# Row of digits and zero of the scan read from PSUM in a radix ranking, with 20 more indirect DMAs beside it

## The reference, cut to what matters

```
gathered = edge_weight[:, None] * h[src]            # 50000 rows
support  = segment_sum(gathered, dst, num_segments=3125)
```

## Time and profile before

| | before |
|---|---|
| median of 3 runs | 6582.15 us (6579.54 to 6584.24) |
| profiled execution, its time | 6588.37 us |
| its span, first to last instruction | 6586.3 us |
| mean granted TensorE clock | 0.885 |
| busy: TensorE, VectorE, GpSimd, ScalarE | 75%, 43%, 35%, 17% |

### The profile page before, as it was taken

One profiled execution on the slowest core, in us unless ns is written; L12 is line 12 of the kernel. 1 busy time (PEld: TensorE's weight loads), 2 busy tenths in 40 slices (PEclk: granted clock), 3 DMA queues, 4 the chain that ended last, 5 costly groups with the idle time before them and its releaser, 6 DMA issues. The chain is left out here.

```text
span 6586.3 us, 86958 instructions
## 1 busy us (share of the span) xinstructions
PE 4944.6 (75%) x21628; PEld 3310.2 (50%) x21677; DVE 2845.9 (43%) x6136; ACT 1150.8 (17%) x2799; POOL 2318.4 (35%) x2417
## 2 busy tenths in 40 slices
PE   4647498979769795776587767496978797979845
PEld 3424376458624684443265434275877443434433
DVE  5575596032330424566696566695242202020142
ACT  2412252012200121111011111012222101010021
POOL 2787302714345042477531577441024000000015
PEclk9999999978879797889898888698979898989957
DMA  0000133435634164699773699673046342414234
GB/s 15 2 1 13 55 140 147 157 111 177 188 128 134 49 200 129 207 305 306 214 241 108 227 306 306 186 268 100 21 132 196 138 138 84 152 60 163 71 80 130
DMA packets 484461, 952.74 MB, mean 145 GB/s; under 512 B 112783, under 2 KB 292602, under 8 KB 481852
## 3 DMA queue, kind: packets, MB, share of 16 engines
q1 hardware_dynamic: 332508, 642.20, 28.8%
q0 software_dynamic: 114208, 281.05, 14.2%
q10 hardware_dynamic: 37568, 27.34, 1.4%
HBM read 733.91 MB, written 216.46 MB: 144 GB/s over the span
## 5 line engine op out<-in xcount | busy, mean ns | idle before, releaser
L1148 PE MATMUL banks<-ring,xn 128*128 128x512 f32 (+1 forms) x3500 | 1355.8, 550 | 143.7 <-DMA ring<-adjacency 143.7
L1148 PEld LDWEIGHTS banks<-ring,xn 128*128 128x128 f32 x3500 | 630.5, 192 | 870.0 <-issue 724.3
L991 POOL DMA_INDIRECT rows<-pairs,idxr x832 | 811.5, 975 | 239.3 <-issue 216.1
L1881 PE MATMUL banks<-agg,hotT 128*128 x1664 | 639.2, 490 | 229.8 <-issue 219.0
L381 POOL DMA_INDIRECT dst_table<-nodes_pay,nodes_row x392 | 379.6, 968 | 643.8 <-DVEq L1116 476.3
L1881 PEld LDWEIGHTS banks<-agg,hotT 128*128 128x128 f32 x1664 | 305.8, 224 | 514.0 <-issue 505.4
L381 POOL DMA_INDIRECT bin_table<-bins_pay,bins_row x392 | 458.7, 1170 | 269.7 <-DVE bins_row L767 119.1
L1854 DVE TENSOR_TENSOR prod<-banks,rows 128x512 f32<-128x512 f32 x416 | 268.0, 686 | 422.7 <-DMA rows<-pairs,idxr 157.4
L1519 POOL MEMSET second<- 64x8192 f32 x1 | 6.9, 6919 | 1204.2 <-POOLq L130 1204.2
L1056 PE MATMUL banks<-spans,lanes 128*128 128x256 f32 x1440 | 332.9, 388 | 119.3 <-DVE spans L1037 107.2
L2346 DVE TENSOR_SCALAR yT<-banks,bs 128x512 f32<-128x512 f32 (+1 forms) x42 | 27.2, 688 | 879.0 <-PE banks L2327 879.0
(11 more groups left out here) (352 smaller groups left out, 6825.2 us busy)
## 6 DMA issues: line engine op xcount, KB each, us to landing
ring<-adjacency SPq DMA_DIRECT2D x150, 1280.0 KB, 5.8
spill<-rows SPq DMA_DIRECT2D x208, 512.0 KB, 5.5
rows<-spill SPq DMA_DIRECT2D x208, 512.0 KB
w1r<-in_L_ffn_W SPq DMA_DIRECT2D x114, 512.0 KB, 3.7
adjacency<-strips SPq DMA_DIRECT2D x13, 3200.0 KB
w1r<-in_L_ffn_w SPq DMA_DIRECT2D x65, 512.0 KB, 3.8
rows<-home_rows SPq DMA_DIRECT2D x35, 640.0 KB
ring<-adjacency SPq DMA_DIRECT2D x25, 640.0 KB, 3.8
```

The source lines that it names most:

```text
L991: nc.gpsimd.indirect_dma_start(rows[:, row, :], None, table, bass.IndirectOffsetOnAxis(ap=idxr[:, at + g:at + g + 1], axis=0))\
L1148: last = nc.tensor.matmul(K.ps[2 * (g % 2) + o][:, 0:wd], x[:, t * D + o * P:t * D + (o + 1) * P], ring[:, n % R, 0:wd // cols, q * SPAN_S ...
L1881: last = nc.tensor.matmul(K.ps[2 + 2 * (jj % 2) + g // 2][:, g % 2 * D:(g % 2 + 1) * D], hotT[:, jj % 2, g * P:(g + 1) * P], tile_of(q, t) ...
```

## The change

The row of digits is copied from SBUF to PSUM bank 7 at the start of each ranking, with a memset of one column there to zero. All comparisons of L564 read the row from PSUM. The scan reads this zero, repeated, as the operand of its maximum, in place of reading `counts` twice; the running sums are never below zero, so the result is the same. VectorE waits for its own copy (`numbered`) ahead of the first comparison. Two of the shares rise: 38 columns instead of 24 beside stage 0 of the nodes' ranking, and 36 instead of 30 beside stage 1. So 29 are left for the layer norm.

```diff
--- before.py
+++ after.py
@@ -541,6 +541,8 @@
     PARTS = 7
     PER_PART = COLS // PARTS
     BF5 = 5
+    WIDEST = max(L, N)
+    digit_iota, nought = K.ps[7][:, 0:WIDEST], K.ps[7][:, WIDEST:WIDEST + 1]
     fills = -(-NB // BF5)
     with stage(nc) as st:
         lo = st.sb("lo", [P, COLS, L], BF)
@@ -549,7 +551,7 @@
         counts = places[:, :, :, :].rearrange("p b d n -> p (b d n)")[:, 0:N * NB]
         counts3 = counts.rearrange("p (n b) -> p n b", b=NB)
         with stage(nc) as st1:
-            made, counted, kept = (st1.sem(x) for x in ("made", "counted", "kept"))
+            made, counted, kept, numbered = (st1.sem(x) for x in ("made", "counted", "kept", "numbered"))
             with nc.Block() as block:

                 @block.gpsimd
@@ -558,11 +560,14 @@

                 @block.vector
                 def _(dve):
+                    nc.vector.memset(nought, 0.0)
+                    nc.vector.tensor_copy(digit_iota, K.iota[:, 0:WIDEST]).then_inc(numbered, 1)
+                    dve.wait_ge(numbered, 1)
                     for part in range(PARTS):
                         at = slice(part * PER_PART, (part + 1) * PER_PART)
                         for hot, width, digit in ((lo, L, low), (hi, N, high)):
                             last = nc.vector.tensor_tensor(
-                                hot[:, at, :], K.iota[:, 0:width].unsqueeze(1).broadcast_to([P, PER_PART, width]),
+                                hot[:, at, :], digit_iota[:, 0:width].unsqueeze(1).broadcast_to([P, PER_PART, width]),
                                 digit[:, at].unsqueeze(2).broadcast_to([P, PER_PART, width]), ALU.is_equal)
                         last.then_inc(made, 1)

@@ -617,7 +622,7 @@
                 def _(dve):
                     link = linker(dve, chain)
                     V = nc.vector
-                    link(V.tensor_tensor_scan(S[:, :], counts, counts, 0.0, ALU.add, ALU.max))
+                    link(V.tensor_tensor_scan(S[:, :], counts, nought.broadcast_to([P, N * NB]), 0.0, ALU.add, ALU.max))
                     link(V.tensor_copy(S_end[:, :], S3[:, :, NB - 1]))
                     link(V.tensor_copy(rc[:, :], S_end[:, :]))
                     V.tensor_tensor(rc[:, 1:N], S_end[:, 1:N], S_end[:, 0:N - 1], ALU.subtract).then_inc(rows, 1)
@@ -929,7 +934,7 @@
                                                   edges.pay[:, :].rearrange("p (c w) -> p c w", w=3)[:, :, 0]))


-SHARES = (104, 24, 30, 156, 12, 6, 11)
+SHARES = (104, 38, 36, 156, 12, 6, 11)
 READY = COLS // 7


```

## The result

The changed kernel took 6544.5 us (median of 4 runs, 6538.21 to 6547.32) beside 6581.74 us for the kernel before (4 runs). The ratio is 0.9942, 95% interval 0.993 to 0.9955: 37 us or 0.6% faster. The forecast was 6544.8 us. The profiled execution took 6547.32 us, its span is 6545.3 us; for before it was 6588.37 and 6586.3, so between the profiles the difference is 41.0 us.

A forecast was written before the change was run, and what follows sets the result against it. POOL's writing of 392 bin-table columns was taken to end stages 0 and 1 and the layer norm. Sum +0.45 - 8.0 - 4.3 - 25.5 = -37.3 us gave 6544.8 us, range 6535 to 6555, chance 0.75.

The forecast's parts named there:

- Parts 1 and 2: Node ranking: digit row in PSUM frees POOL in stage 0, -8.0 us; scan's zero in PSUM in stage 1, -4.3 us.
- rival (b): Second SBUF input is not what holds POOL, length could be; nothing released, +1.0 us, 6583.2 us; chance 0.06.
- Price of the PSUM operand: Start of each ranking: copy, memset and wait cost 0.45 us; the 28 comparisons were taken as unchanged.
- rival (c): Comparisons: a PSUM input repeated by stride zero is read more slowly; at twice the time +38.2 us, 6620.4 us; chance 0.04.
- The 65 ns more for each instruction: Skill's higher fixed cost of a PSUM source, on 28 comparisons and 2 scans: 1.9 us in all; not in the forecast.
- Rival (a): Comparisons let POOL go, the scan doesn't: stage 1 +7.7 us in place of -4.3, 6556.9 us; chance 0.11.
- Handovers: Next engine starts 0.68 us after ScalarE or 0.88 after VectorE, instead of 2.82 or 3.14 us after POOL.
- Stage 1: Node ranking, scan to TensorE: VectorE instead of POOL ends it, 6 added columns hidden, -4.3 us.
- the layer norm: 29 instead of 49 columns are left there; 20 x 1.275 = -25.5 us.
- Behind 737 us: Eight layers after the sort: unchanged; a rival had the gain given back there, under 13 us gained (0.03) or a loss (0.01).
- their cover is ScalarE's tail: Stage 0, node ranking: the 14 added columns cost nothing behind ScalarE's end; without that cover 17.9 us.

The follow-up runs named there:

- row, scan, zero in SBUF: Changed kernel with the digit row from SBUF (ratio 0.9981), the scan reading counts twice (0.9952), or the scan's zero in SBUF (0.9999, slow chip).
- the first experiment: Changed kernel, but the comparisons read the row of digits from SBUF again: 6575.60 us, ratio 0.9981 to the kernel before.
- the fuller kernel: Changed kernel with shares 40, 42, 158 and the PSUM copy only in the ranking of nodes: 7605.91 us (ratio 0.9979), again 7602.32 us (0.9982).

## Why the prediction was right

**Parts 1 and 2, what holds POOL: right.** The prediction read from the mix of columns in stage 2 that an input in PSUM frees POOL. Three kernels show it from both sides (row, scan, zero in SBUF), and the changed kernel's own trace settles rival (b): a comparison of 3.89 us and a scan of 20.57 us leave POOL alone, so length is not the cause. That also decides against what the prediction weighed for this rival in the Trainium skill ("SBUF — State Buffer", section "Who interferes with whom"): that `tensor_tensor` was not seen to stall DMA. Issuing these indirect DMAs it does stall, by up to 3.4 us a column (4.41 against 0.97 in the first experiment). The prediction took one half of that paragraph only; the other half says that with both inputs in SBUF `tensor_tensor` contends with what GpSimd reads there, and these runs agree with it.

**Price of the PSUM operand: right.** The comparisons went from 3072 to 3060 ns and from 3888 to 3879, with the PSUM row repeated by stride zero; rival (c) is out. The copy and the memset overlap and delayed the start of stage 0 of the nodes by 0.2 us where 0.45 was taken. The 65 ns more for each instruction, an estimate worked out from the Trainium skill ("VectorE: DVE Perf Modes", section on the TRN2 errata), don't show.

**Rival (a), the scan keeps its hold: wrong**, at 21 free columns.

**Handovers: right in kind.** Of the 12.7 us gained in stages 0 and 1, 4.4 had been put down to POOL no longer being the last at the barrier. ScalarE to VectorE took 319.51 - 318.48 = 1.0 (0.68 taken), VectorE to TensorE 404.93 - 404.04 = 0.9 (0.88 taken).

**Stage 1, -4.8 for -4.3.** VectorE's own chain is 0.5 us shorter, 84.5 instead of 85.0 us from the scan to its end; half of that is one cast that lasted 403 ns before and 180 after. POOL's own end was 3.6 us earlier than the prediction's sum has it (387.9 for 399.5 - 8.0), which costs or gives nothing behind VectorE: two columns passed beside the fifty instructions before one was held, where the sum had the first one wait.

**The term that was mis-sized: the layer norm.** The 20 columns gave 25.5 us exactly (35.70 us from first to last start against 61.18), but the gap from POOL's last column to the read shrank from 5.99 to 4.36 us, which the prediction held fixed. Its 1.6 us are most of the 2.1 by which the sum missed. The old shares with the new operands have the 49 columns and the long gap again (717.66 + 0.97 to 724.61, 6.0 us), so it goes with the columns and not with the operands.

**Behind 737 us: nothing given back.** The rest of the span moved by 1.6 us, the other way. That the forecast meets the median within 0.3 us is luck: the sum was 2.1 us short, and the profiled execution of before stood 6.6 us over its median, that of after 2.8.

**What the prediction did not have at all** is that the cover of the moved columns was not there in the later sets. Its words were "their cover is ScalarE's tail". On the slow kind of chip TensorE, which feeds ScalarE, stands while POOL issues; the cover is gone, and stage 0 is 16.1 us longer for 14 columns, 1.15 us each on the mean (1.2 for each of the two more in the fuller kernel), nearly the 1.275 a column costs in the layer norm. What is left there are stage 1 and the rest of the layer norm's gain: 9 to 12 us by the medians instead of 37.

## What to carry to other kernels

Where GpSimd issues indirect DMAs beside long VectorE work, look at the lengths of its instructions against one that runs alone; if they follow VectorE's, put one of VectorE's two inputs in PSUM (one row, or one column, repeated, is enough), and only then move issues under that work. Here the first half alone gave some 12 us and the second nothing; both gave 37 on one kind of chip, and 9 to 12 on the other. Before counting such issues as hidden beside TensorE, check on more than one chip that TensorE still gets its instructions.

## What the runs showed of the hardware that was not expected

- In three of the five sets the kernels took 7602 to 7665 us (medians) instead of 6545 to 6588. In them TensorE was idle for up to 53 us at a time while GpSimd issued indirect DMAs back to back, and one packet of the instruction queue q8 came in 219 us instead of 11 in 200. Without the columns the stage was as fast as elsewhere (206.3 us). Why the packets come beside GpSimd's DMAs in some sets and not in others was not found. Of the 1045 us between the two profiles of the kernel before, 312 arise before the table is read (1048.96 against 737.00); the 733 behind it were not taken apart.
- There, a held GpSimd leaves TensorE and ScalarE alone: before, with the comparisons holding it, stage 0 lasted 64.0 and 64.1 us on the two kinds of chip.
- A GpSimd instruction can wait through many short VectorE ones: fifty of 0.34 us held one column for 14.0 to 15.0 us in every run looked at, though the two or three in front of it passed beside the same instructions. What lets those pass stays open.
- The barrier behind a stage that GpSimd ends last costs more with more issues in it: 2.8 us behind 24 columns, 3.8 and 4.2 behind 38. With the last landing in it, the gap was 5.3 behind 19 columns (slow kind of chip), 4.4 to 4.8 behind 29, 6.0 behind 49 and 12.4 behind 177. So it isn't a plain function of the count; what it is was not settled.
- The fuller kernel (40, 42, 158) had the lowest median in both of its sets, 8 and 5 us under the changed one; the intervals of the two ratios overlap, so the order is likely and not sure. On the kind of chip of the first result it was not measured; the 42 columns in stage 1 are hidden even on the slow kind (TensorE 85.4 to 85.9 us after the scan), and the 40 in stage 0 should be, at 263.97 + 39 x 1.275 + 0.97 = 314.7 and a handover of up to 4.2 us, against the scan's start at 319.5 that ScalarE's end allows: that is argued, not shown.
